# A selective scan's states summed into y by two DMA transfers a state instead of one

## The reference

```python
# expert layer: 8 experts, 128 -> 512 -> 128, all of them computed for each token
h = silu(einsum('bsh,ehf->ebsf', x, w_gate)) * einsum('bsh,ehf->ebsf', x, w_up)
out = einsum('ebsh,bse->bsh', einsum('ebsf,efh->ebsh', h, w_down), cw)   # cw: from two softmaxes
# mamba block: 256 channels d, 16 states n, scan over the 1024 tokens t of a batch row
xs, z = split(x @ W_in);  xc = silu(conv4(xs) + conv_b);  dt, B, C from xc @ W_x
h[t] = exp(dt * A) * h[t-1] + (dt * xc) * B[t]
y[t] = sum over n of h[t, :, n] * C[t, n]    +  xc * D
return (y * silu(z)) @ W_out
```

## Time and profile before

| | us |
|---|---|
| median of three runs (1424.75, 1426.55, 1426.56) | 1426.55 |
| the profiled execution's own time | 1428.13 |
| its span, from the first to the last instruction | 1426.3 |
| TensorE matmul busy | 1302.3 (91%) |
| VectorE busy | 1196.2 (84%) |
| ScalarE busy | 862.9 (61%) |
| GpSimd busy | 369.6 (26%) |
| mean busy share of the 16 DMA engines, first GpSimd's queue, then SyncE's | 34.1%, 29.8% |
| mean granted TensorE clock | 0.976 |

### The profile page before, as it was taken

One profiled execution on the slowest core, in us unless ns is written; L12 is line 12 of the kernel. 1 busy time (PEld: TensorE's weight loads), 2 busy tenths in 40 slices (PEclk: granted clock), 3 DMA queues, 4 the chain that ended last, 5 costly groups with the idle time before them and its releaser, 6 DMA issues.

```text
span 1426.3 us, 15239 instructions
## 1 busy us (share of the span) xinstructions
PE 1302.3 (91%) x4752; PEld 862.3 (60%) x4752; DVE 1196.2 (84%) x1770; ACT 862.9 (61%) x1301; POOL 369.6 (26%) x332
## 2 busy tenths in 40 slices
PE   6999898998889889998898989899989989898898
PEld 4666565665556656565565656666656656565665
DVE  4555799899898998999989999898989999998343
ACT  5436666767755675666758676577646576563322
POOL 0111222323322241333313232223322232221201
PEclk9999999999999999999999999999999999999899
DMA  6421676567676767765885868667767766888122
GB/s 188 99 52 47 146 172 153 140 153 158 160 161 150 155 144 176 156 159 133 182 185 110 177 149 194 152 149 153 166 150 173 155 150 162 167 194 171 38 52 45
DMA packets 105938, 205.93 MB, mean 144 GB/s; under 512 B 12801, under 2 KB 25601, under 8 KB 105857
## 3 DMA queue, kind: packets, MB, share of 16 engines
q0 software_dynamic: 32256, 92.29, 34.1%
q1 hardware_dynamic: 73600, 112.68, 29.8%
HBM read 109.77 MB, written 2.88 MB: 79 GB/s over the span
## 4 chain that ended last, share of the span: by engine, by line
PE 32%; DMA 20%; ACT 18%; DVE 17%; issue 10%; POOL 2%; SPq 1%; POOLq 0%; DVEq 0%; ACTq 0%
DMA Y<-HS 17%; PE PS L663 10%; PE PS L608 7%; PE PS L610 6%; PE PS L609 6%; DVE HS L869 5%; ACT DA L1004 4%; DVE HB L797 4%; ACT L933 3%; ACT HB L933 3%; ACT L1004 3%; DMA XT<-in_L_attn_x_dram 2%; DMA ACC<-YE 2%; DVE HS L880 2%; DVE HS L859 1%
## 5 line engine op out<-in xcount | busy, mean ns | idle before, releaser
L933 ACT ACTIVATE HB<-PS 128x512 f32<-128x512 f32 x512 | 297.6, 596 | 423.2 <-PE PS L610 421.4
L663 PE MATMUL PS<-HB,WD 128*128 128x512 f32 x1024 | 531.3, 601 | 0.0
L797 DVE TENSOR_TENSOR HB<-PS,HB 128x512 f32<-128x512 f32 x512 | 347.1, 678 | 118.8 <-ACT HB L933 64.0
L608 PE MATMUL PS<-XH,WG 128*128 128x512 f32 x512 | 382.4, 747 | 66.8 <-ACT HB L933 65.4
L1062 POOL DMA_DIRECT2D Y<-HS x128 | 111.8, 873 | 557.0 <-DMA Y<-HS 320.9
L608 PEld LDWEIGHTS PS<-XH,WG 128*128 128x128 f32 x512 | 98.2, 192 | 234.5 <-ACT HB L933 183.0
L608 PE MATMUL PS<-XH,WU 128*128 128x512 f32 x512 | 209.8, 410 | 24.9 <-DVE HB L797 24.6
L663 PEld LDWEIGHTS PS<-HB,WD 128*128 128x128 f32 x1024 | 193.9, 191 | 43.2 <-issue 1.0
L610 PE MATMUL PS<-XH,WU 128*128 128x512 f32 x512 | 204.0, 398 | 0.0
L610 PE MATMUL PS<-XH,WG 128*128 128x512 f32 x512 | 203.9, 398 | 0.0
L609 PE MATMUL PS<-XH,WU 128*128 128x512 f32 x512 | 202.6, 396 | 0.0
(11 more groups left out here) (111 smaller groups left out, 1243.5 us busy)
## 6 DMA issues: line engine op xcount, KB each, us to landing
BCB<-BCD SPq DMA_DIRECT2D x128, 512.0 KB, 5.4
Y<-HS POOLq DMA_DIRECT2D x128, 512.0 KB, 7.3
CWB<-CWD SPq DMA_DIRECT2D x128, 256.0 KB, 4.4
ACC<-YE POOLq DMA_DIRECT2D x96, 256.0 KB, 5.4
XT<-in_L_attn_x_dram SPq DMA_DIRECT2D x8, 256.0 KB, 4.2
WD<-in_L_ffn_w_down_dram SPq DMA_DIRECT2D x8, 256.0 KB, 6.1
out_dram<-XT SPq DMA_DIRECT2D x8, 256.0 KB, 2.4
HS<-in_L_ffn_w_gate_dram SPq DMA_DIRECT2D x6, 256.0 KB, 4.8
```

The lines of the kernel that those rows point to most:

```text
L608: pe.matmul(o, w[0], m[0], start=first, stop=False)
L663: pe.matmul(expert(g), WD[:, e, c, :], HB[:, i % NH, :], start=c == 0, stop=c == FC - 1).then_inc(S["m_dn"], 1)
L797: v.tensor_tensor(H, up(i), H, ALU.mult).then_inc(S["v_h"], 1)
L933: a.activation(HB[:, i % NH, :], gate(i), ACT.Silu).then_inc(S["a_sil"], 1)
```

## The change

Each state's sum is issued as two transfers, one for each half of the channels (128 partitions x 512 f32), each with a semaphore of its own, `c_y0` and `c_y1`. A half waits only for the same half of the state before. Those who waited for `c_y` (line 859, line 886) now wait for both. The planner books 0.9 us of GpSimd for each half and 5.5 us until it has landed. In `norm`, a caller that will use RM now gets the lock `rm` before it takes the PSUM bank for its transposition; `before` used to take the lock after it. That `before` waits for a free lock ahead of its norm is as it was.

```diff
-    def norm(b, what):
+    def norm(b, what, rows=False):
...
         yield from until(at + 0.7)
+        while rows and rm["lock"]:
+            yield False
+        if rows:
+            rm["lock"] = True
         bk = yield from take()
         at = step("ln_t", q, bk, pe=.6)
...
-        q, b, at = yield from norm(t % XR, ("x1", t))
-        while rm["lock"]:
-            yield False
-        rm["lock"] = True
+        q, b, at = yield from norm(t % XR, ("x1", t), rows=True)
...
-    y_at = [0.0]
+    y_at = [0.0, 0.0]
...
-            clock["p"] = max(clock["p"], at, y_at[0]) + .9
-            y_at[0] = clock["p"] + 6.5
+            for j in range(2):
+                clock["p"] = max(clock["p"], at, y_at[j]) + .9
+                y_at[j] = clock["p"] + 5.5
...
-        scanned[t] = y_at[0]
+        scanned[t] = y_at[1]
...
                     if m >= HR:
-                        wt.wait_ge(S["c_y"], 16 * (m - HR + 1))
+                        for j in range(2):
+                            wt.wait_ge(S[f"c_y{j}"], 16 * (m - HR + 1))
...
-                    wt.wait_ge(S["c_y"], 16 * NS * (t + 1))
+                    for j in range(2):
+                        wt.wait_ge(S[f"c_y{j}"], 16 * NS * (t + 1))
...
-                    if m:
-                        wt.wait_ge(S["c_y"], 16 * m)
-                    gp.dma_start(Y[:, t % 2, :, :], HS[:, m % HR, :, :], accum_op=ALU.add).then_inc(S["c_y"], 16)
+                    for j in range(2):
+                        if m:
+                            wt.wait_ge(S[f"c_y{j}"], 16 * m)
+                        gp.dma_start(Y[:, t % 2, j, :], HS[:, m % HR, j, :], accum_op=ALU.add).then_inc(S[f"c_y{j}"], 16)
```

More of the change, by code:

```diff
@@ L459, in macaron_program @@
         S = {}
-        for n in ("c_small c_con c_acc c_y c_bcd c_cwd o_x init w_hi w_lo dv "
+        for n in ("c_small c_con c_acc c_y0 c_y1 c_bcd c_cwd o_x init w_hi w_lo dv "
                   "m_g m_u m_dn m_tr m_lg m_tz m_win m_wx m_wt m_wo "
```

## The result

| | before | after |
|---|---|---|
| median of 20 runs each, us | 1426.93 | 1430.62 |
| lowest to highest | 1424.75 to 1429.59 | 1425.11 to 1438.91 |
| profiled execution's own time (span) | 1428.13 (1426.3) | 1429.23 (1427.4) |

The ratio is 1.0022, with a 95% interval of 1.0012 to 1.0033: the change makes the kernel some 3.1 us slower, where 3.0 us faster was forecast. That it is slower is clear of the noise; whether it is beyond the 0.2% that the prediction named as its bound is not, for the interval reaches to both sides of it. The value lies in the range, the sign is wrong.

A forecast was written before the change was run, and what follows sets the result against it. VectorE's order up to the last state, a last transfer into Y and an untouched tail were taken as the bound. Terms of -3.6 and +0.6 gave -3.0 us, a median of 1423.6 us, range 1416 to 1432 us.

The forecast's parts named there:

- The bound and the map: Whole kernel: VectorE's order up to the last state, one last transfer into Y, then a tail the change leaves alone.
- Part 1: Second issue on GpSimd: 0.87 us a state, 112 us more, covered by idle time; smaller packets 0.2 us a state, hidden.
- part 4: GpSimd's pieces behind the second issue: the layer norm's power, awaited at L741, charged 0.6 us, from 0 to 2.6.
- Part 2: Pace of successive sums into Y: from 7.8 to 6.2 us a state, halves landing in 5.4; backlog goes.
- the closing from which the sum took most: Tile 1's closing product, L886: its transfer was late behind its predecessor; 1.75 us of its 3.23 us wait were to go.
- Part 3: VectorE's waits for Y at the closing products: 3.6 us less; last half's landing taken as 0, between -1.0 and +0.5.
- The term of -3.6 us: VectorE's waits at the closings of tiles: 1.75 + 0.65 + 0.85 + 0.32 us less, counted in full.
- I take 0: Landing of the last half at a closing: no change taken, with -1.0 to +0.5 us kept as range.
- rival B: Transfers into Y serialize on the engines, late states gain only the 0.5 us gap: 1426.5 us, chance 15%.
- Part 5: Planner's new booking and lock edit: pieces and a transposition move slightly, costed at 0, between -3 and +5 us.
- Rival C: New order places VectorE's pieces less well, four more waits at L797 cost 4.7 us: 1431 us, chance 23%.

The follow-up runs named there:

- e17: Kernel before with GpSimd's elementwise instructions cut from 512 columns to 16, one transfer a state: 1404.27 us, ratio 0.9849 to before.
- e18: e1 (two transfers a state, order and booking of before) with GpSimd's elementwise instructions cut to 16 columns: 1405.07 us, ratio 0.9848 to before.
- e2: Changed kernel's plan, lock edit and booking, but the single transfer a state of before: 1427.55 us, ratio 1.0020 to before.
- e8: Kernel before with the two half transfers and the lock edit, but the booking of before: 1419.35 us, ratio 0.9942 to before.
- e3: Kernel before with the lock edit alone, one transfer a state: 1422.57 us, ratio 0.9971 to before.
- e1: Kernel before with only the two half transfers, their semaphores and waits; plan of before: 1430.31 us, ratio 1.0036 to before.
- e6: Kernel before with each half of Y padded by 16 bytes, so the one transfer goes in 256 packets of 2 KB: 1431.62 us, ratio 1.0034.

## Why the prediction was wrong

**The bound and the map.** Right: VectorE's order up to the last state, then a fixed tail. In all kernels the end follows the start of tile 7's closing product by 104 to 109 us.

**Part 1.** The terms were right: 0.88 us an issue, 33% of GpSimd, 50688 packets, 36.2% of the queue. The cover was not. "Covered while GpSimd's idle time is there" looked at GpSimd alone. The issue does not cost GpSimd's time; it moves GpSimd's elementwise pieces against VectorE's, which are lengthened by what they overlap. Halves added 2.5 us to VectorE in the order of before, 2.3 in the lock's (1191.6 to 1193.9), 2.6 in the changed one (1194.6 to 1197.2). In the order of before, e17 and e18 show that halves cost nothing without GpSimd's long pieces. The prediction priced what waits behind the second issue (part 4, 0.6 us at L741, where it stayed at 4.2 us), and not what runs beside it.

**Part 2.** The forecast pace was 6.2 us a state. The halves land in 6.6 us, not 5.4. The expert sum was the nearest row, but a half has its twin in flight with it; that this is the reason was not tried by itself. The backlog did shrink (58 late issues to 40), but not at the closing from which the sum took most:

```profile
441.86 1.23 DVE L884 TENSOR_TENSOR HS<-BCB,HS 128x1024 f32<-128x1024 f32 x1
445.63 0.87 POOL L1068 DMA_DIRECT2D Y<-HS  x1 [5.47 <-DMA Y<-HS]
446.73 0.86 POOL L1068 DMA_DIRECT2D Y<-HS  x1 [0.23 <-DMA Y<-HS]
...
454.45 1.22 DVE L891 TENSOR_TENSOR Y<-Y,SZ 128x1024 f32<-128x1024 f32 x1 [1.86 <-DMA Y<-HS]
```

This is tile 1 after the change. Both halves are late behind their predecessors, by 2.5 and 3.6 us from the end of L884, where one transfer was late by 2.05. From the end of the last state to the closing product it is 11.36 us, and was 11.13; VectorE's own wait there is shorter, 1.86 us against 3.23, only because it came later.

**Part 3.** The term of -3.6 us was mis-sized. Halves alone took 0.8 us off the closings' waits in the order of before (9.7 to 8.9) and added to them in the other two (3.2 to 4.3, 3.8 to 6.9). "I take 0" for the last half was too kind: two halves are whole 7.7 us after the first issue against 7.3. In the full plan halves were forecast at -3.0 us and are worth +0.2 in a thousand (e2 to after), 0.3 us, with some 2 us of noise either way. So far the mechanism of rival B fits, though its sign, a landing of over 7 us for a half, did not come. The rule that the prediction quoted from the Trainium skill, DMA: Bandwidth & Descriptors, "Rules for kernel authors", says of disjoint halves of the partitions that two transfers serialize over the same engines. This trace agrees for halves inside each partition: two are not whole sooner than one, at 7.7 against 7.3 us.

**Part 5** failed by about as much. The order was costed at 0, between -3 and +5 us, with the words that the lock moves a transposition "by a microsecond". With one transfer a state the whole new order costs 2.0 in a thousand (e2), 2.9 us. These 2.9 and the 3.3 us by which the halves missed are the way from 3.0 us faster to 3.1 slower. And the 2.9 is a small rest of large terms that the prediction did not see. In the plan the lock moves 533 of 1397 VectorE steps and is worth -2.9 in a thousand (4 us) by itself; the booking on top of halves and lock costs 8.0 (11 us). Rival C had the direction, the mechanism in outline (the new order puts VectorE's pieces less well) and nearly the value (1431), but the value was luck: it came from four more waits of 1.18 us at L797, and those waits rose by 19 us. Nor do they mark the slower kernels. In e8, which is faster than before, the two stand at 132.8 us and in e3 at 129.6, both above the 118.1 of before:

```profile
DVE HB L798 <- PE PS L611: 71.3, 60, 3.6
DVE HB L798 <- ACT HB L936: 61.5, 53, 4.3
```

What tells the orders apart is VectorE's wait for the output product where tile 4 closes, 4.2 us in before and 0.2 in e8, which the prediction did not read.

**The parts were taken as additive.** They are not: the same two transfers cost 3.6 and gain 2.9 in a thousand in two orders. Why they gain in the lock's order, with VectorE 2.3 us busier and no less waiting for Y, stays open; e3 and e8 were not timed on the same chip, and their intervals just overlap (0.9960 and 0.9955).

## What to carry to other kernels

Idle time of an engine is a cover only for work that disturbs nobody: when an engine gets more to do, look at what its next instructions will then run beside, and which of those pairs slow each other. An edit to a planner is an edit to the kernel's order and wants to be measured apart from the change of mechanism that it comes with; here the best kernel was the change without its booking. Look for the wait that separates faster orders from slower ones in one stretch, with the granted clock beside it, before the sum over all waits.

## What the runs showed of the hardware

- An elementwise GpSimd instruction and a VectorE instruction with all operands in SBUF lengthen each other (a scan of 1.27 us took 2.72 with 1.60 us of overlap, a sum of GpSimd 2.05 instead of 1.27); a VectorE product with one operand in PSUM was not lengthened. With GpSimd's instructions cut to 16 columns VectorE was busy 46.9 us less, of 1196.2, and the kernel ran 22 us faster (1404.27 against 1426.27).
- The issue of an adding transfer on GpSimd costs 0.87 us for 128 rows of 4 KB and 1.21 us for 256 pieces of 2 KB in one transfer, but 0.88 us for each of two transfers with 128 rows of 2 KB: here it went by pieces and not by bytes. In the traces of before and e1 no VectorE instruction beside an issue alone was lengthened.
- Two adding transfers of 256 KB in flight at once land in 6.6 us each on the median under this load, and both together 7.7 us after the first issue; one of 512 KB lands in 7.3, and in 7.2 when its packets are of 2 KB (e6).
- TensorE's granted clock was 1.00 through an idle time of 3.0 us and the 0.8 us of work behind it, and then 0.50 to 0.51 for 10.3 us in which it was busy throughout.
